# Making the bf16 high parts of a group's weights on GpSimd instead of ScalarE, and preparing them four slots earlier

## The reference, cut to what matters

```python
x = x + attention(layernorm(x), ctx)      # 8 groups, 2 heads each, d = 128; self and cross attention
x = x + ffn(layernorm(x))                 # SiLU(gate) * up, then down; hidden size 1408
# inside attention, per group g:
q, k, v = fp8_linear(ln(x));  qx = fp8_linear(ln(x));  kx, vx = ctx @ w_kv_x
q, k, qx, kx = ln(each head)
core = softmax(q k^T / sqrt(d)) v         # likewise the cross part with kx, vx
out = fp8(clamp(concat(core, xout) / smooth)) @ wproj
```

## Time and profile before

| | |
|---|---|
| time, median of 3 runs | 1767.88 us (1767.86 to 1768.89) |
| the profiled execution's own time | 1770.42 us |
| its span | 1768.6 us |
| busy, TensorE / VectorE / ScalarE / GpSimd | 1661.4 / 1391.3 / 1378.8 / 1108.7 us |
| instructions of GpSimd | 1031 |
| granted TensorE clock, mean | 0.989 |

### The profile page before, as it was taken

One profiled execution on the slowest core, in us unless ns is written; L12 is line 12 of the kernel. 1 busy time (PEld: TensorE's weight loads), 2 busy tenths in 40 slices (PEclk: granted clock), 3 DMA queues, 4 the chain that ended last, 5 costly groups with the idle time before them and its releaser, 6 DMA issues.

```text
span 1768.6 us, 44139 instructions
## 1 busy us (share of the span) xinstructions
PE 1661.4 (94%) x15776; PEld 1229.8 (70%) x15776; DVE 1391.3 (79%) x3199; ACT 1378.8 (78%) x2955; POOL 1108.7 (63%) x1031
## 2 busy tenths in 40 slices
PE   1559999999999999999999999999999989999999
PEld 1437788888888888888888888888878544444444
DVE  8999999999899999989998999998779753323232
ACT  6879999999999999999999999999999623121221
POOL 1357777787787778777877877787778513021212
PEclk9979999999999999999999999999999999999999
DMA  5937787787888788888877887777999980213000
GB/s 174 219 94 130 149 151 143 143 150 143 146 144 155 145 143 152 141 142 144 150 143 146 145 156 145 139 141 129 170 203 196 198 232 24 98 46 118 25 24 24
DMA packets 663556, 241.46 MB, mean 137 GB/s; under 512 B 619440, under 2 KB 635952, under 8 KB 662832
## 3 DMA queue, kind: packets, MB, share of 16 engines
q1 hardware_dynamic: 662048, 230.20, 66.7%
q0 software_dynamic: 1296, 8.52, 2.3%
HBM read 75.15 MB, written 29.51 MB: 59 GB/s over the span
## 4 chain that ended last, share of the span: by engine, by line
ACT 39%; PE 26%; POOL 17%; issue 9%; DVE 6%; DMA 2%; SPq 2%; ACTq 0%; POOLq 0%; DVEq 0%
POOL local L1081 13%; ACT local L987 12%; ACT local L917 9%; ACT local L984 8%; ACT local L904 4%; PE ps_s L668 4%; PE ps_pj L661 3%; POOL head_rstd L1058 3%; PE ps_pj L793 2%; PE ps_pj L794 2%; PE ps_s L807 2%; PE ps_s L808 2%; PE ps_o L793 2%; PE ps_o L794 2%; ACT v_hi L907 2%
## 5 line engine op out<-in xcount | busy, mean ns | idle before, releaser
L1081 POOL TENSOR_TENSOR local<-local 128x512 bf16<-128x512 f32 x512 | 593.7, 1160 | 287.4 <-ACT local L987 287.1
L661 PE MATMUL ps_pj<-wide 128*128 128x256 bf16 (+1 forms) x5544 | 583.5, 254 | 5.7 <-DVE wide L1157 4.0
L661 PEld LDWEIGHTS ps_pj<-wide 128*128 128x128 bf16 x5544 | 469.0, 98 | 112.9 <-DVE wide L1157 4.4
L984 ACT ACTIVATE local<-ps_s,neg_max 128x512 f32<-128x512 f32 x512 | 408.4, 798 | 28.9 <-DVE neg_max L1318 28.6
L987 ACT ACTIVATE local<-ps_s,neg_max 128x512 bf16<-128x512 f32 x512 | 411.8, 804 | 0.0
L708 PE MATMUL ps_o<-v_hi,local 128*128 128x129 bf16 x2048 | 375.6, 221 | 5.4 <-DMA local<-local 3.3
L710 PE MATMUL ps_o<-v_hi,local 128*128 128x129 bf16 x2048 | 375.2, 219 | 0.0
L709 PE MATMUL ps_o<-local 128*128 128x128 bf16 x2048 | 375.1, 218 | 0.0
L1318 DVE TENSOR_REDUCE neg_max<-ps_s 128x1 f32<-128x512 f32 x512 | 343.6, 671 | 11.5 <-PE ps_s L728 11.3
L917 ACT ACTIVATE local<-ps_pj,head_rstd 128x128 f32<-128x128 f32 x756 | 243.9, 453 | 53.6 <-issue 51.9
L1058 POOL TENSOR_TENSOR head_rstd<-sq_sum,minus_half 128x3 f32<-128x3 f32 x256 | 250.0, 977 | 28.9 <-DVE sq_sum L1233 28.9
(11 more groups left out here) (122 smaller groups left out, 2669.5 us busy)
## 6 DMA issues: line engine op xcount, KB each, us to landing
quantised_heads<-local SPq DMA_DIRECT2D x128, 128.0 KB, 2.5
w_raw<-w_group SPq DMA_DIRECT2D x56, 256.0 KB, 3.2
wide<-quantised_heads SPq DMA_DIRECT2D x3, 4096.0 KB, 13.5
local<-local SPq DMA_TRANSPOSE x640, 3.2
wide<-packed_weights SPq DMA_DIRECT2D x32, 256.0 KB, 3.2
wide<-x SPq DMA_DIRECT2D x7, 1024.0 KB, 8.7
packed_weights<-w_proj POOLq DMA_DIRECT2D x4, 1024.0 KB, 15.1
wide<-quantised_heads SPq DMA_DIRECT2D x16, 256.0 KB, 3.5
```

The source lines that it names most:

```text
L661: last = mm(dst[:, at:at + n], lhs, w_at(par, part, c, cross * 512 + at, n), start=(k == 0), stop=(k == len(terms) - 1))
L984: a(p_exp[:, u % 2], ps_s[u % 2][:], ACT.Exp, bias=neg_max[:, u % 4:u % 4 + 1])
L1081: tt_(pp[:, u % PP_BUFS, 1], p_exp[:, u % 2], pp[:, u % PP_BUFS, 0], ALU.subtract)\
```

## The change

The high parts of chunks 8 to 31 are no longer made by ScalarE's activation but by a GpSimd `tensor_scalar` (add 0.0, float32 in, bf16 out, 128x512), again in two halves. GpSimd emits them last in their slot, behind the low part of the probabilities and the power. Both bases move four slots earlier; the first half moves one more. So sums run in slot 11, the scaling in 14, 15, 2 and 3, the halves in 3 and 5, the low part in 7; loads start in slot 12 and 14 instead of 0 and 2. Chunks 4 to 7 stay on ScalarE at their old slots.

```diff
-        PREP = {"sums": 3, "scale0": 6, "scale1": 7, "scale2": 10, "scale3": 11, "hi0": 12, "hi1": 13, "lo": 15}
-        PREP_BASE = (-20, -4, 12, 28)
+        PREP = {"sums": 3, "scale0": 6, "scale1": 7, "scale2": 10, "scale3": 11, "hi0": 11, "hi1": 13, "lo": 15}
+        PREP_BASE = (-24, -8, 8, 24)
-        LOAD_BASE = (-32, -16, 0, 16)
+        LOAD_BASE = (-36, -20, -4, 12)
...
-                    for half in range(2):
+                    for half in range(2 if first else 0):
                         for n in prep_at(g, slot, f"hi{half}"):
+                            if n >= 2 * CH:
+                                continue
...
+            def weight_hi(par, c, count, half):
+                pool.wait_ge(w_scaled, count)
+                pool.sem_inc(waited_pool, 1)
+                at, end = half * GW // 2, (half + 1) * GW // 2
+                done = nc.gpsimd.tensor_scalar(w_par(par, c * GW + at, end - at), raw(c)[:, at:end], 0.0, None, ALU.add)
+                if half == 1:
+                    done.then_inc(w_hi_done, 1)
...
                     for k in tile_at(slot, VAR_LAG, first, last):
                         head_power(tile_place(k)[1], GROUP_TILES * g + TILES + k)
+                    for half in range(2):
+                        for n in prep_at(g, slot, f"hi{half}"):
+                            if n >= 2 * CH:
+                                weight_hi(n // CH % 2, n % CH, n + 1, half)
```

More of the change, by code:

```diff
@@ L235, in block_kernel @@
         waited_sp = sem("waited_sp")
+        waited_pool = sem("waited_pool")
         smooth_in = sem("smooth_in")
```

## The result

The changed kernel takes 1785.20 us (1783.64 to 1787.72, 4 runs) against 1767.87 us; the ratio is 1.0096 (95% interval 1.0084 to 1.0109). It is slower by 1%. The forecast was 1764.9 us, a gain of 3.0 that a measurement can hardly tell from no change, with a range from 1759 to 1773 and a chance of 0.22 for slower. The profiled execution is the fastest of the four, 1783.64 us with a span of 1781.8.

A forecast was written before the change was run, and what follows sets the result against it. TensorE was taken to set the pace, 39.70 of 40.54 us a cycle. Loss 0.84 to 0.70 over 24 chunks gives 3.4, plus 0.3 behind them, minus 0.3 start and 0.4 overrun: gain 3.0, 1767.9 to 1764.9 us, range 1759 to 1773.

The forecast's parts named there:

- What bounds the kernel: Cycle of 16 slots: TensorE alone needs 39.70 of 40.54 us; other engines can give at most 0.84 us.
- Both halves leave ScalarE, 0.63 in slot 9 comes back: Slots 8 and 9: without the halves on ScalarE, TensorE's slot 9 loses nothing, worth 0.63 us a cycle.
- Second half to GpSimd: Slot 5: the half takes 0.75 us (0.54 to 1.16) and hides in GpSimd's 0.83 us gap before slot 6.
- The term for the overrun: Gap before slot 6: a half up to 0.87 us overruns by 0.04 in 24 cycles; 0.4 us taken.
- The rival with the slow half: Slots 5 to 8: a half of 1.16 us overruns by 0.33, slot 8 loses 1.03, total 1772.5 us; chance 0.20.
- First half free: Slot 3: the first half on GpSimd is hidden by the 1.32 us gap before slot 4's low part of the probabilities.
- The low part in slot 7 holds the power up by 0.98 us, slot 8 loses 0.70: Slots 7 and 8: the collision delays GpSimd's power by 0.98 us, so TensorE loses 0.70 us in slot 8.
- One input on GpSimd: GpSimd halves: the skill's line rate for one input gives 0.43 us for 512 columns, and both halves fit.
- The low part beside GpSimd: Slot 7: by the exclusive port lock, the moved low part costs 0.98 us wherever it meets the power.
- The low part in slot 11 costs TensorE nothing: Slot 11 before the change: GpSimd's delay of 0.98 us makes only a head norm late; no `qk_rest` follows.
- The rest of the table: Scaling, sums and loads meet nothing new after moving; only chunk 8's first load is tight, 0.3 us once.
- The same cycle as before: Whole cycle: a chain through ScalarE closes at 40.54 us whatever TensorE does, total stays 1767.9 us; chance 0.12.

The follow-up runs named there:

- the short piece: The changed kernel with plain DMAs for the transposing ones and the second GpSimd piece of each chunk cut from 512 to 16 columns: 1760.75 us, ratio 0.9962.
- the control of before: The kernel before the change with its 640 transposing DMAs replaced by plain DMAs of the same bytes: 1762.19 us, ratio 0.9963.

## Why the prediction was wrong, by its own steps

- **What bounds the kernel: right.** TensorE's 39.70 us a cycle and the 0.84 us lost in slots 8 and 9. Two kernels reach 39.70 in their cycles with preparation, and the changed kernel in the first two without it (1230.15 and 1269.85).
- **Both halves leave ScalarE, 0.63 in slot 9 comes back: right.** Slot 9 is at 2.64.
- **Second half to GpSimd: this step failed.** "From above: GpSimd's two-input instructions of 128x512, 1.09 and 1.16 us" was taken as a bound, and of the new instruction it says that it "computes less than the select, so I take 0.75 us". The instruction takes 1.50 us, above both. The reasoning was that one input and one simple operation can't take longer than two inputs, or than a select. The run with tensor_copy shows where it fails: the number of inputs doesn't set the duration. Reading one tensor and writing one takes 0.61 us there, and 1.50 with tensor_scalar and an addition of zero. The term for the overrun is 0.67 us a cycle (1.50 - 0.83) instead of at most 0.04, 24 times, some 15 us. The rival with the slow half had the mechanism and the turning point (0.97 us) right; its price was computed at 1.16 us, since nothing larger was thought possible, and with 1.50 in its place it gives 24 x (1.37 - 0.84) = 13 us slower.
- **First half free: wrong, small.** 1.50 us in a gap of 1.32 leaves 0.14 us of lateness, which is still there in slot 6 and costs 24 x 0.14 = 3.4 us. The second half's own part is 0.59; together that is 0.73, a little more than the 0.67 by the durations.
- **The low part in slot 7 holds the power up by 0.98 us, slot 8 loses 0.70: right.** 0.71 with tensor_copy, 0.75 with the short piece; and with tensor_copy and the low part in slot 11 nothing is left.
- **One input on GpSimd.** The Trainium skill (GPSIMD Engine Reference, Engine selection) calls one-input work on GpSimd "roughly line-rate". The trace comes near it for tensor_copy (612 ns against the prediction's estimate of 430) and disagrees for tensor_scalar (1497 ns). The measurement decides, and it depends on the instruction.
- **The low part beside GpSimd.** The Trainium skill (SBUF — State Buffer, Who interferes with whom) has the second to come wait for the first. The traces agree where the low part comes first (GpSimd's instruction behind it takes 2.04 us instead of 1.16) or comes 0.06 to 0.23 us into a GpSimd instruction of 128x512 (it shows 2.0 to 2.2 us). They disagree where it comes 0.17 us behind the power: 1.22 and 0.85 us, neither delayed. So "by that rule the moved low part costs the same 0.98 us wherever it meets the power" was wrong. Why the power and the low part can overlap in that order isn't settled.
- **The low part in slot 11 costs TensorE nothing: by the traces wrong, but hidden.** It is 0.25 us a cycle, seen once slots 8 and 9 lose little else.
- **The rest of the table.** Loads: nothing in the cycles. The start: 0.3 taken, 1.6 us measured, of which 1.3 where chunk 8 is summed in slot 43 and waits for its load; the prediction called this place tight, and took too little for it.
- **The same cycle as before**, a rival at 0.12, is refuted: with both halves still on ScalarE the cycle reaches 39.70.

## What to carry to other kernels

A bound "from above" must come from the same instruction, or from a reason that excludes more; a nearest neighbour of another kind is a guess, and a forecast whose sign turns at 0.97 us should have left room above 1.16. Before moving work to another engine, look at what is released right behind its new place: here 0.73 us of lateness in one slot became some 0.75 us of TensorE's time in each cycle, since a score product waits for the work just behind. And the cheaper fix was next door: the same work on the engine that had it, in the idle places of slot 9, took 13 us off the control of before.

## What the runs showed of the hardware that was not expected

- GpSimd turns 128x512 float32 into bf16 in 612 ns with tensor_copy (medians of 48 each), 1163 ns with tensor_tensor, 1497 ns with tensor_scalar (one operation, immediate operand). tensor_scalar of 128x16 takes 0.26 us, so (1.50 - 0.26)/496 = 2.5 ns a column.
- A VectorE tensor_tensor with two SBUF inputs (128x1024) takes 1.22 us with GpSimd idle, or beside GpSimd's power of 128x3 that began 0.17 us before it (0.85 us, not delayed). When it comes 0.06 to 0.38 us into a GpSimd instruction of 128x512 it shows 1.85 to 2.2 us. In each of these latter cases GpSimd's next instruction is held, too (0.85 becomes 1.83 to 1.86 us), and so is one of 128x512 that begins 0.19 us behind it (1.16 becomes 2.04).
